# Attention heads in the two row halves of TensorE, four slots of keys and queries

## The reference

```python
scale = sqrt(N_HEADS / dm)
q = split(x @ W_q.T)
k = split(x @ W_k.T)
v = split(x @ W_v.T)
attn = jax.nn.softmax(scale * jnp.einsum('bnqd,bnkd->bnqk', q, k), axis=-1)
o = jnp.einsum('bnqk,bnkd->bnqd', attn, v)
o = o.transpose(0, 2, 1, 3).reshape(b, l, dm)
return o @ W_o.T
```

## Time and profile before

| what | value |
|---|---|
| median of 3 runs | 754.28 us (752.54 to 757.0) |
| the profiled execution | 751.72 us |
| its span on the core | 749.9 us |
| PE, DVE, ACT, POOL busy | 86%, 58%, 52%, 8% |
| granted TensorE clock, mean over the span | 0.93 |
| DMA packets | 34483, 45.12 MB |

### The profile page before, as it was taken

How to read it: one execution, slowest core, us unless ns; L and a number is a source line. 1 busy time by engine, 2 the same in 40 slices (tenths; PEclk the granted TensorE clock), 3 DMA queues, 4 the chain that set the end, 5 groups by cost and what they waited for, 6 DMA issues and landing times.

```text
span 749.9 us, 9940 instructions
## 1 busy us (share of the span) xinstructions
PE 643.5 (86%) x3426; PEld 431.1 (57%) x3426; DVE 432.8 (58%) x860; ACT 393.6 (52%) x748; POOL 59.1 (8%) x89
## 2 busy tenths in 40 slices
PE   2855698799979989899889989799799988899896
PEld 1411577354468767544478777544478776544585
DVE  0451595688165754877165755876275747783344
ACT  1432477156773564367764474267755573368710
POOL 2010220300000002200000003100000004000000
PEclk9966699689989999899999999799999999799999
DMA  8996330521000005220000005220000004220000
GB/s 286 381 379 222 113 112 29 105 38 31 2 0 1 1 19 104 63 44 3 0 1 3 1 29 105 51 44 3 0 1 1 1 15 91 51 44 2 1 1 29
DMA packets 34483, 45.12 MB, mean 60 GB/s; under 512 B 4736, under 2 KB 27392, under 8 KB 34304
## 3 DMA queue, kind: packets, MB, share of 16 engines
q1 hardware_dynamic: 29728, 31.32, 14.9%
q0 software_dynamic: 3488, 10.49, 4.9%
q10 hardware_dynamic: 1216, 2.66, 1.4%
HBM read 28.45 MB, written 3.15 MB: 42 GB/s over the span
## 4 chain that ended last, share of the span: by engine, by line
PE 65%; DVE 12%; DMA 9%; ACT 8%; issue 3%; SPq 2%; ACTq 1%; DVEq 0%
PE psum L1214 31%; PE psum L1374 9%; PE psum L1447 8%; PE psum L1436 7%; DVE mx L1031 3%; DMA arena<-in_hyp_w 3%; DMA kst<-split 2%; DMA early_pieces<-in_hyp_w 2%; PE psum L1475 2%; SPq L306 1%; PE psum L1200 1%; ACT arena L713 1%; PE psum L1302 1%; PE psum L1336 1%; DMA qst<-mrow_lo 1%
## 5 line engine op out<-in xcount | busy, mean ns | idle before, releaser
L713 ACT ACTIVATE arena<-psum 128x512 f32<-128x512 f32 x256 | 141.7, 600 | 88.7 <-PE psum L1436 87.5
L1031 DVE TENSOR_REDUCE mx<-psum 128x1 f32<-128x512 f32 x256 | 162.3, 683 | 41.5 <-PE psum L1374 41.2
L1374 PE MATMUL psum<-kst,qst 96*128 96x512 f32 x192 | 87.7, 507 | 21.1 <-DMA kst<-split 10.5
L1214 PE MATMUL psum<-act,ghw_hi 128*128 128x512 f32 (+1 forms) x288 | 93.8, 390 | 3.1 <-DVE act L832 1.7
L1436 PE MATMUL psum<-qst,kst 98*128 98x512 f32 x192 | 82.2, 450 | 2.2 <-ACT arena L713 1.3
L1374 PEld LDWEIGHTS psum<-kst,qst 96*128 96x128 f32 x192 | 42.5, 224 | 60.4 <-DVE mx L1031 35.7
L1214 PE MATMUL psum<-upw_hi,kst 128*128 128x512 f32 x256 | 72.4, 404 | 1.2 <-issue 1.2
L1447 PE MATMUL psum<-arena,vals 128*17 128x512 f32 x512 | 68.8, 609 | 1.3 <-ACT arena L713 1.0
L1214 PEld LDWEIGHTS psum<-act,ghw_hi 128*128 128x128 f32 x288 | 56.0, 204 | 14.7 <-DVE act L832 3.2
L433 POOL DMA_DIRECT2D kst<-split x36 | 17.7, 497 | 492.9 <-DMA kst<-split 412.0
L1214 PE MATMUL psum<-act,ghw_lo 128*128 128x512 f32 (+1 forms) x144 | 55.0, 385 | 0.0
(11 more groups left out here) (184 smaller groups left out, 1075.3 us busy)
## 6 DMA issues: line engine op xcount, KB each, us to landing
early_pieces<-in_hyp_w SPq DMA_DIRECT2D x17, 512.0 KB, 9.3
arena<-in_hyp_w SPq DMA_DIRECT2D x15, 512.0 KB, 9.2
qst<-split SPq DMA_DIRECT2D x72, 64.0 KB, 3.4
kst<-split POOLq DMA_DIRECT2D x36, 128.0 KB, 3.6
arena<-in_up_w POOLq DMA_DIRECT2D x8, 256.0 KB, 5.6
arena<-in_x SPq DMA_DIRECT2D x4, 512.0 KB, 3.8
arena<-in_gh_w POOLq DMA_DIRECT2D x8, 256.0 KB, 3.5
out_x<-arena SPq DMA_DIRECT2D x8, 256.0 KB, 2.1
```

The source lines that it names most:

```text
L713: s.activation(probs[:, kb % 2, i, :], bank[3 + n % RING], ACT.Exp).then_inc(a_p, 1)
L1031: v.reduce_max(mx[:, g % 2, col:col + 1], bank[u % RING], AX.X).then_inc(d_max, 1)
L1214: ins = pe.matmul(dst, lhs(a, c), rhs(z, c), start=start and n == 0, stop=stop and n == len(terms) - 1, skip_group_check=skip)
L1374: pe.matmul(bank[u % RING], qst[g % 3][0:KROWS, i, P * t:P * t + P], keys_of(g)[0:KROWS, i // 2, :], start=True, stop=True).then_inc(e_max, 1)
```

## The change

**Layout.** A head now has 48 rows (3 x 16), 50 with the two of the maximum. Heads 0 and 2 of a group lie from row 0, heads 1 and 3 from row 64, in two columns of tiles; keys and queries have the same layout. No row is zero, and a matmul uses 48 or 50 rows, from row 0 or from row 64. **Order of the heads.** `max_order` makes the max tiles alternate between heads of the upper and the lower rows, odd head first; the scores alternate as they did, even head first, so that a max tile and the score behind it lie in opposite halves from k = 6 of group 0 on. The numbers of tiles and their places in the stream are unchanged. **Slots.** There are four key slots and four query slots (the fourth is half of `act_both`), so nothing is written twice in a batch; the ones are set once in all. `inp`, in which other stages hold their input, moves from `kst` to `qst`. **Copies.** For group 0 ACT issues the high keys (2 copies of 64 KB), POOL the others (4); SP issues the 6 of the queries, high parts first, and no longer waits for the low parts to do so. POOL issues all other keys at once, 6 copies of 64 KB for a group. The maximum's row goes out in two pieces, one for each half: for group 0 two from ACT and two from SP, for the others two from SP and two from POOL (`odd_rows`, L451 of the new file).

```diff
-KROWS = 3 * 32
+HALF_ROWS = 64
+KROWS = 3 * DH
 SROWS = KROWS + 2
...
-        kst = [sb(f"kst{i}", [P, G // 2, L], F32R) for i in range(3)]
-        qst = [sb(f"qst{i}", [P, G, L], F32R) for i in range(2)] + [act_both]
-        inp = kst[0:2]
+        kst = [sb(f"kst{g}", [P, G // 2, L], F32R) for g in range(NG)]
+        qst = [sb(f"qst{g}", [P, G // 2, L], F32R) for g in range(NG - 1)] + [act_both[:, 0:G // 2, :]]
+        inp = qst[1:3]
...
+        def rows_of(tile, i, rows):
+            at = HALF_ROWS * (i % 2)
+            return tile[at:at + rows, i // 2, :]
+        def stacked(tile, e, k):
+            at = HALF_ROWS * e + DH * k
+            return tile[at:at + DH, :, :].bitcast(F32)
+        def max_order(r):
+            return 2 * (r // (2 * T)) + 1 - r % 2, r // 2 % T
...
             def stack_q(b, g):
                 if g == 0:
-                    sp.wait_ge(queries_zero, 2)
+                    sp.wait_ge(a_qk, b * 4 + 2)
+                if g == 1:
+                    sp.wait_ge(a_qk, b * 4 + 4)
+                    sp.wait_ge(d_qk, b * 4 + 4)
-                if g >= 3:
-                    sp.wait_ge(e_score, b * (NG * T * G) + T * G * (g - 2))
-                if g == 2:
-                    sp.wait_ge(act_zero, b + 1)
+                if g == 3:
+                    sp.wait_ge(e_maxT, b * NG + 1)
+                for k, part in ((0, 0), (2, 0), (1, 1)):
+                    if g == 0 and part == 1:
+                        sp.wait_ge(d_qk, b * 4 + 2)
+                    for e in range(2):
+                        sp.dma_start(stacked(qst[g], e, k), rows_in_split(g, e, part, 0)).then_inc(queries_in[g], 16)
...
+            def odd_rows(b, g):
+                pool.wait_ge(a_mrow, b * NG + g + 1)
+                pool.sem_inc(keys_free, 1)
+                pool.dma_start(maxima_row(g, 0, 1), maxima_of(0, 1)).then_inc(odd_rows_in, 16)
+                pool.wait_ge(d_mrow, b * NG + g + 1)
+                pool.sem_inc(keys_free, 1)
+                pool.dma_start(maxima_row(g, 1, 1), maxima_of(1, 1)).then_inc(odd_rows_in, 16)
...
-                for i in range(2):
-                    pool.memset(kst[i][KROWS:SROWS, :, :].bitcast(F32), 1.0).then_inc(keys_ones, 1)
-                pool.memset(qst[2][:, :, :].bitcast(F32), 0.0).then_inc(act_zero, 1)
...
+                    if u % (G * T) == 0:
+                        pe.wait_ge(queries_in[g], b * (6 * 16) + 6 * 16)
...
-                    pe.matmul(bank[u % RING], qst[g % 3][0:KROWS, i, P * t:P * t + P],
-                              keys_of(g)[0:KROWS, i // 2, :], start=True, stop=True).then_inc(e_max, 1)
+                    pe.matmul(bank[u % RING], rows_of(qst[g], i, KROWS)[:, P * t:P * t + P],
+                              rows_of(kst[g], i, KROWS), start=True, stop=True).then_inc(e_max, 1)
...
-                    pe.matmul(bank[3 + k % RING], keys_of(g)[0:SROWS, i // 2, P * kb:P * kb + P],
-                              qst[g % 3][0:SROWS, i, :], start=True, stop=True).then_inc(e_score, 1)
+                    pe.matmul(bank[3 + k % RING], rows_of(kst[g], i, SROWS)[:, P * kb:P * kb + P],
+                              rows_of(qst[g], i, SROWS), start=True, stop=True).then_inc(e_score, 1)
```

More of the change, by code:

```diff
@@ L67 @@
 AT_ALPHA, ALPHA_OUT = 0, 3
-HEAD_ORDER = (0, 2, 1, 3)
 RING = 3
@@ L151, in build, with rows_in_split, maxima_row, maxima_of @@
         hh_s = [[split[:, 2 * p + n, :] for n in range(2)] for p in range(2)]
-        def keys_of(g):
-            return kst[(g + 2) % 3]
-        def maxima_row(g, k):
-            row = qst[g % 3][KROWS + k:KROWS + k + 1, :, :].rearrange("p i (t n) -> p (i t) n", t=T)
-            return row.bitcast(F32)
+        def rows_of(tile, i, rows):
[4 more added lines that the diff above has]
+            return tile[at:at + DH, :, :].bitcast(F32)
+        def rows_in_split(g, e, part, first):
+            at = 32 * g + DH * e
+            return split[at:at + DH, 4 * part + first:4 * part + first + 2, :].bitcast(F32)
+        def maxima_row(g, k, e):
+            at = HALF_ROWS * e + KROWS + k
+            return qst[g][at:at + 1, :, :].rearrange("p i (t n) -> p (i t) n", t=T).bitcast(F32)
+        def maxima_of(k, e):
+            return mrow[k][2 * T * e:2 * T * e + 2 * T, :].bitcast(F32)
+        def max_order(r):
+            return 2 * (r // (2 * T)) + 1 - r % 2, r // 2 % T
+        def max_column(i, t):
+            return (i % 2) * 2 * T + (i // 2) * T + t
         def cut(first_col, columns, **dims):
@@ L220, in build @@
         keys_free = sem("keys_free")
-        queries_in = [[sem(f"{e}_queries_in{i}") for i in range(3)] for e in ("even", "odd")]
-        keys_lo_in, keys_hi_in = sem("keys_lo_in"), sem("keys_hi_in")
-        keys_in = [sem(f"keys_in{i}") for i in range(3)]
+        queries_in = [sem(f"queries_in{g}") for g in range(NG)]
+        keys_hi_in = sem("keys_hi_in")
+        keys_in = [sem(f"keys_in{g}") for g in range(NG)]
+        odd_rows_in = sem("odd_rows_in")
         hblk_set = sem("hblk_set")
-        queries_zero = sem("queries_zero")
-        act_zero, keys_ones = sem("act_zero"), sem("keys_ones")
+        keys_ones = sem("keys_ones")
         rows_in, out_done = sem("rows_in"), sem("out_done")
@@ L388, in batch @@
                                  ).then_inc(x_in, 16)
-                sp.wait_ge(a_qk, b * 4 + 2)
-                sp.wait_ge(d_qk, b * 4 + 2)
-                for g in range(2):
+                for g in range(3):
                     stack_q(b, g)
                 maxima_rows(b, 0)
-                stack_q(b, 2)
+                stack_q(b, 3)
                 if not first:
@@ L452, in _ @@
                 if n == LATE + STAGES - 1:
-                    for i in range(2):
-                        pool.memset(qst[i][:, :, :].bitcast(F32), 0.0).then_inc(queries_zero, 1)
+                    for g in range(NG):
+                        pool.memset(kst[g][:, :, :].bitcast(F32), 1.0).then_inc(keys_ones, 1)
             pool.wait_ge(pool_ready, POOL_READY)
-            pool.wait_ge(queries_zero, 2)
+            pool.wait_ge(keys_ones, NG)
             def kept_low(b, k):
@@ L473, in batch @@
                     kept_low(b, 1)
[L474 to L482 removed]
                 stack_k(b, 3)
+                for g in range(1, NG):
+                    odd_rows(b, g)
             batch(0, first=True)
@@ L644, in batch @@
                                  ).then_inc(a_qk, 1)
-                def first_keys(parts, ready, signal):
-                    s.wait_ge(ready, b * 4 + 4)
-                    for k, part in parts:
-                        src = split[0:32, 4 * part + 2:4 * part + 4, :]
-                        s.dma_start(keys_of(0)[32 * k:32 * k + 32, :, :].bitcast(F32), src.bitcast(F32)
-                                    ).then_inc(signal, 16)
-                first_keys(((0, 0), (1, 0)), a_qk, keys_hi_in)
+                s.wait_ge(a_qk, b * 4 + 4)
+                if first:
+                    s.wait_ge(keys_ones, NG)
+                for e in range(2):
+                    s.dma_start(stacked(kst[0], e, 0), rows_in_split(0, e, 0, 2)).then_inc(keys_hi_in, 16)
                 for h in range(2):
-                    if h == 1:
-                        first_keys(((2, 1),), d_qk, keys_lo_in)
                     s.wait_ge(e_v, b * 2 + h + 1)
@@ L702, in batch @@
                 s.wait_ge(a_mrow, b * NG + 1)
-                s.dma_start(maxima_row(0, 0), mrow[0][:, :].bitcast(F32)).then_inc(rows_in, 16)
+                for e in range(2):
+                    s.dma_start(maxima_row(0, 0, e), maxima_of(0, e)).then_inc(rows_in, 16)
                 if not first:
```

76 lines of the change are left out of this document (30 added, 46 removed).

## The result

The changed kernel takes 773.8 us (median of 4 runs) against 754.08 us before. Medians in this document are over all runs, ratios leave out the few in a slower state of the chip, here one of 782.4 us: the ratio is 1.0243, 95% interval 1.0203 to 1.0283. The kernel is slower, by 2.4%, where 1.0% was forecast. The profiled execution took 769.73 us, its span is 767.9 us against 749.9, so 18.0 us are to be found.

What follows compares the result with a forecast made beforehand. PE's stream was taken as the bound from first burst to the last with max tiles, DVE before. Terms -10.9 + 13.2 + 2.4 + 1.8 + 0.6 + 0.8 = +7.9 us took 751.72 to 759.6, median 762 us; range 744 to 778.

Steps and rivals of the forecast that it cites:

- the overlap: Attention steps with max tiles: max tile and following score run side by side, 3.04 to 2.7 us per step, saving 10.9 us.
- rival C: Attention: tiles in opposite halves don't run side by side, steps stay 3.04 us; +6.8 us, 761 us; chance 0.12.
- no gain ahead of the first burst: Attention before the first burst of `weigh`: nothing gained, since the loop there runs over DVE and ACT.
- the lower clock in the attention, by rows: Attention: with half the rows at work, PE's clock stays low through first burst and two more steps; 13.2 us, four batches.
- Rival A: Attention: PE's clock returns as before the change, first step after first burst 2.7 us; -7.7 us, 746.6 us; chance 0.30.
- The extra low steps: Attention, where alphas delay DVE or in last scores: one more step at low clock in two of four batches, 2.4 us.
- the first copies: Before each batch's first max tile: more bytes ahead but an earlier start, net 0, with -0.8 to +1.0 us a batch.
- the changes of form: Kept work, batches 1 to 3: switching between 128-row and 64-row tiles, less paired tiles' saving; 0.6 us a batch, 1.8 total.
- the maximum rows: Ahead of batch 0's first score: SP issues two row copies instead of one, 0.6 us; in later batches kept work covers it.
- The 0.8 us for group 3's row: At group 3's first score: PE waits 0.2 us more for the maximum's row, half now from POOL; 0.8 us, four batches.

## Why the prediction was right and wrong

**Right: the overlap.** A score starts in the same instant as its max tile, the step shown is 2.7 us as worked out, and rival C falls. The term of 10.9 us stands against at least 7.8 measured between the kernels with 64 and with 128 rows, 5.2 of them behind the first burst, where the term lies. By the bursts at the higher clock it is about 12 us, an estimate: 3.1 us less in the steps from the second burst on that have max tiles and 0.7 in the first one, with 0.8 lost in the last two steps, in each batch.

**Wrong: no gain ahead of the first burst.** I wrote that this stretch gains nothing, as its loop runs over DVE. The halves overlap there too, and it is 5.4 us shorter over the four batches (2.6 us shorter with 64 rows than with 128, which have the better clock). That is luck for the total: it cancels as much as the fallen clock ahead of the turn costs (5.5 us, below).

**Right: the lower clock in the attention, by rows.** In batch 0 the clock was still at 0.53 from 157 to 160 us, a low step took 334.60 - 330.75 = 3.85 us where 3.9 was forecast, and the mean fell below 0.93. Rival A falls. The forecast took 13.2 + 2.4 = 15.6 us for this. Behind the first burst the whole is +3.2 us, so with the 12 of the overlap the lower clock costs about 15, an estimate from the same steps; the kernel with 64 rows gives back 10.6, all of it in batches 1 to 3 (batch 0: 53.57 and 53.72 us), where I had expected it in all four. The extra low steps came in every batch and not in two. Overlap and clock together were forecast at +4.7 us and measured, with the gain ahead of the first burst, at -2.2.

**Wrong: the first copies, the term set to 0 with bounds of -0.8 to +1.0 us.** This is the step that failed. In batch 0, the batch I read it in, it holds: first max tile 0.6 us later. In batches 1 to 3 PE waits 3.5 us where it waited 1.9, 5.0 us in the three. Held back, the later copies take 3.2 of these away (waits of 2.38, 2.47 and 2.56 us): POOL's are new there and no longer held behind the first ones, in a stretch where the DMA share is 0.93. The other 1.8 us stay with the first group's own copies, all six of the queries and not three. I wrote of both, and set their price to nothing against the earlier start.

**Wrong: what that wait does to the clock.** The prediction looked for a fallen clock around the first scores, and nowhere ahead of them. Behind PE's idle time of 3.5 us the kept work runs at 0.50 for some 6 us in batches 1 and 3, and for half of that in batch 2. First max tile to turn takes 53.60 us in batches 1 to 3, and would take 46.5 at clock 1.00 (3 x 15.5), so 7.1 us of low clock against 1.55 before (42.23 - 3 x 13.56): 5.5 us, all of it in batches 1 and 3. The kernel with the 128-row filling runs at 1.00 there in all three batches, and the one with 32 rows does not. This is shown for the filled and the unfilled wait; the length of the wait alone does not decide it, as two waits of 3.3 us passed without a fall. That the wait is also what lowers the clock in the batches behind is not: filled, they took 60, 61 and 54 us.

**Mis-sized: the changes of form,** 0.6 us in a batch, measured 1.95, at the upper bound (1.9). The change into a max tile costs 0.10 us as assumed, the one out of it 0.29 over two steps, while tiles side by side save their 0.2 us a pair as assumed. In three batches 5.9 us against 1.8. The upper end, 5.7 us, was the better estimate.

**Mis-sized: the maximum rows,** 0.6 us in batch 0 (measured 0.8), and for batches 1 to 3 "kept work lies over it". It does not: turn to first score takes 1.2 us longer in each, 0.6 of that behind ACT's second issue, which delays the last kept tile. The rest is not taken apart by any run; the changes of form lie in it, and a clock of 0.63 where it was 0.71 to 0.81. The 0.8 us for group 3's row did not come: PE waited 0.39 and 0.47 us for it in batches 1 and 2 before, and in no batch of the changed kernel.

Together: start 0.6, wait 5.0, kept work 11.5, turn to score 4.4, attention -2.2, and -1.3 that the stretches outside the attention and the end differ by, 18.0 us. The forecast had 0, 0, 1.8, 0.6, 5.5 and 0 in these places, 7.9 us. The sign was right for a reason that was only half of it: the attention itself, to which I charged most of the loss, became 2.2 us shorter, and the loss lay ahead of it.

## What to carry to other kernels

A transfer that is freed from a wait can share the DMA engines with the transfers that someone is waiting for; when slots come free, price that, or keep the order by a wait on the first ones (here 1.1 us off a wait of 3.5). Packing matmuls into fewer rows has a second price beside the change of form: here the clock was held less well with fewer rows at work, so try zeros in unused rows, and full-row matmuls in a wait of the 2 to 3.5 us seen here, if dense work follows at once. The first is clear of noise in the changed kernel, the second in the kernel before (3 us of 752). And where the clock moves, judge an edit by its stretch as well as by the whole: 0.6 us saved ahead of a sensitive stretch can disappear in it.

## What was not expected of the hardware

- Twelve matmuls of 32 rows kept PE as busy as twelve of 128 rows (3.00 and 2.89 of 3 us), and the clock fell behind the first and not behind the second.
- Rows of zeros in the keys raised the clock in the attention from 0.84 to 0.92 in the same stretch, at no cost in time of the single tile.
- Leaving a 64-row tile for a 128-row one costs three times what entering it costs, 0.29 against 0.10 us, and a third of that shows only at the step behind.
- The same stretch of the same instructions took 53.9 or 60.5 us within one execution, by the clock alone (0.92 and 0.78).
- Two copies of 8 x 128 issued one behind the other on ACT's queue took 1.39 us where one of 16 x 128 took 0.53.
- The halves gain 1.0 to 1.6 us a batch ahead of the first burst, at the lower clock.
